# Letting the first expert's blocks start ahead of the last row's scatters, and writing later experts' pads between experts

## The chip, the cores and the metric

The kernel runs on one core of a Trainium2 chip. The metric is the device time of one execution in microseconds (us), taken as the median of several runs. Engines are named as in the profile: PE (TensorE), DVE (VectorE), ACT (ScalarE), POOL (GpSimd), SP (SyncE); a "q" behind a name (SPq, ACTq) is that engine's instruction queue, which also issues DMAs and reads registers.

## The reference

Everything is in float32, on x of 8 batch rows x 512 tokens x 128. Four parts follow one another, each of them added to x:

```python
x = x + attn_a(layernorm(x))          # 16 heads of 64, causal softmax
x = x + ffn(layernorm(x))             # mixture of experts, below
x = x + attn_b(layernorm(x))          # linear attention, 8 heads of 128, then a gated MLP
x = x + ffn(layernorm(x))             # the same mixture, the same weights

def ffn(x):                            # E = 8 experts, the best K = 2 of each token
    xn = layernorm(x) * gamma + beta
    scores, idx = top_k(softmax(xn @ Wr + br), 2)
    full = [relu(xn @ W1[e] + b1[e]) @ W2[e] + b2[e] for e in range(8)]   # 128 -> 512 -> 128
    c = relu(b1) @ W2 + b2                                              # one vector per expert
    out = sum over the 2 chosen of scores * (full[idx] - c[idx] + c.sum())
    return x + out
```

So the mixture runs twice in one execution. Each time 4096 tokens x 2 choices = 8192 token rows are spread over 8 experts, unevenly.

## The kernel before

The kernel computes only the chosen experts. Each token's row of 130 floats (128 of data, the token's number and its first expert) is **scattered** to a DRAM buffer `expert_in`, in which every expert has a region of its own (`REGION` = 4352 rows). POOL does this with indirect DMAs, 8 for each batch row (`Route.pool_scatter_one`, L674 to L677). The semaphores `scattered[u]` count what has landed; batch row b uses number b mod ring (ring 2 in the first mixture, 3 in the second), so the last row, 7, shares number 1 with other rows in both.

When the last row is routed, PE sums the counts of all experts with one matmul (`pe_count`, L914), and DVE makes the plan of them (`dve_plan`, L921): where each region ends (`fill_at`) and how many blocks of 256 rows each expert has (`blocks`). The last block of an expert is rarely full. So ACT writes 256 rows of padding behind each region's end, one DMA of 130 KB per expert (`fill`, L940), each with its own semaphore `filled[e]`; all eight are issued ahead of ACT's part of the experts.

Then every engine runs `each_block` (L896): for each expert in turn a hardware loop over its blocks. Only SP reads an expert's number of blocks as it comes to it (L900); PE, ACT, DVE and POOL read all eight numbers beforehand (`load_counts`, L889 to L894). For one block:

- SP loads it from `expert_in` to the one tile `xb` (L955), once the block before it is transposed and its token numbers are copied. SP is thus about two blocks ahead of ACT.
- PE, in this order: the matmuls to the hidden layer (L979), the transposes of the *next* block (L973), the matmuls back (L989). A wait in L973 holds up L989 of the block before it.
- ACT applies relu (L1000), DVE copies the meta columns (L1011), scales the transposed block (L1015) and adds the constant (L1035), and POOL scatters the result to `expert_out` (L1047).

SP's waits are `rows_written` (L958), all scatters of all rows, once before the first block, and `pads_written(e)` (L962), the pad of expert e, ahead of that expert's blocks.

In the first mixture DVE, PE and ACT also fold weights for the next stage between the plan and the experts (`Folding`): for DVE these are `dve_c`, `dve_const`, then `load_counts`, then `dve_last` (L831 to L846), which ends with two copies of the experts' constants (L841) and the subtraction that makes `WVO_lo` (L845). PE waits for L841's second copy before its experts. In the second mixture nothing stands between the plan and the experts but `load_counts`. POOL's `pool_work` begins with `prime` (L470), two small DMAs whose landing it waits for.

## Time and profile before

| | us |
|---|---|
| median of 3 runs (lowest, highest) | 1390.03 (1387.22, 1393.89) |
| the profiled execution, time | 1388.27 |
| its span | 1386.4 |
| PE, DVE, ACT, POOL busy in the span | 1232.6, 925.7, 822.6, 516.3 |

How to read it: the span is cut into stages by the instructions' lines. Attention a runs from 0 to about 541 us, the last row's routing and the folding to 577, the first mixture's experts to about 712, linear attention to about 1050, the MLP and the routing to 1214, the second mixture's experts to about 1359, and the last combination to the end. The shares of busy time are averages over stages with different limits. In the rows further down, a line of the timeline gives the start, the length of the piece, the engine, the line of the kernel, what is written from what, how many instructions, and in brackets how long the engine had been idle before it and what ended that. "issue" there is time in which the engine's queue itself was at work or waited for nothing that the profile shows.

### The profile page before, as it was taken

How to read it: one execution, taken by the hardware profiler on the slowest of the kernel's cores; microseconds unless marked ns; L12 is line 12 of the kernel's file. 1: busy time of each engine (PE TensorE's matmuls, PEld its weight loads, DVE VectorE, ACT ScalarE, POOL GpSimd, SP SyncE). 2: the span in 40 equal slices, each digit the busy share in tenths (PEclk: the TensorE clock that was granted, in tenths of full speed). 3: DMA queues.
4: the chain of work that ended last, by engine and by line, in shares of the span. 5: the costliest groups of instructions: out<-in, count | busy, mean ns of one | idle time of the engine just before them, and what ended most of it. 6: DMA issues, size and time to landing. Idle time of an engine off the chain costs nothing. (4 is left out here: it accounts for less than half of the span.)

```text
span 1386.4 us, 27110 instructions
## 1 busy us (share of the span) xinstructions
PE 1232.6 (89%) x7787; PEld 930.6 (67%) x7787; DVE 925.7 (67%) x3602; ACT 822.6 (59%) x2478; POOL 516.3 (37%) x683
## 2 busy tenths in 40 slices
PE   6999999999999998699958999999997988199990
PEld 5666666666666666499945777777774655189990
DVE  6778888888888776344436888888773555344445
ACT  5888888888888885244423555555654654044440
POOL 2112333342424233355532344434332455535451
PEclk9999999999999999799988999999998998589995
DMA  9100000000000000222220000000000011222225
GB/s 283 47 1 1 9 9 9 9 9 11 11 8 13 7 13 11 72 69 71 70 89 16 16 17 16 16 1 1 1 1 1 24 32 33 64 63 73 68 71 189
DMA packets 54445, 52.92 MB, mean 38 GB/s; under 512 B 7341, under 2 KB 43098, under 8 KB 54330
## 3 DMA queue, kind: packets, MB, share of 16 engines
q1 hardware_dynamic: 36320, 29.39, 7.3%
q0 software_dynamic: 8928, 17.84, 3.8%
q10 hardware_dynamic: 9082, 4.33, 1.1%
q8 instruction: 52, 0.85, 0.3%
q14 instruction: 63, 0.52, 0.1%
HBM read 29.48 MB, written 22.05 MB: 37 GB/s over the span
## 5 line engine op out<-in xcount | busy, mean ns | idle before, releaser
L1350 ACT ACTIVATE prob<-prob,negmax 128x512 f32<-128x512 f32 (+3 forms) x512 | 283.0, 556 | 78.7 <-DVE negmax L1449 76.7
L1449 DVE CUSTOM_DVE_ANT_0 prob<-bank,mask 128x512 f32<-128x512 f32 (+3 forms) x512 | 227.8, 483 | 51.0 <-PE bank L1159 50.7
L1526 POOL TENSOR_TENSOR Vs<-Vh_sb,rinv 128x256 f32<-128x256 f32 x128 | 78.2, 611 | 364.1 <-DVE rinv L1426 363.9
L1047 POOL DMA_INDIRECT expert_out<-f_x_yb,f_x_to x142 | 136.1, 958 | 155.1 <-DVE f_x_yb L1035 88.0
L1176 PE MATMUL bank<-prob,Vs 128*64 128x512 f32 (+3 forms) x1024 | 151.9, 439 | 0.9 <-DVE zT_lo L1421 0.9
L675 POOL DMA_INDIRECT expert_in<-f_xn,f_slot x128 | 127.0, 993 | 47.7 <-issue 29.3
L979 PE MATMUL bank<-f_x_xbT,W_sb 128*128 128x256 f32 x568 | 138.5, 388 | 1.6 <-DVE f_x_xbT L1015 1.5
L1000 ACT ACTIVATE f_x_hid<-bank,cols 128x256 f32<-128x256 f32 x144 | 63.4, 473 | 93.0 <-PE bank L979 93.0
L979 PEld LDWEIGHTS bank<-f_x_xbT,W_sb 128*128 128x128 f32 x568 | 104.6, 194 | 14.8 <-DVE f_x_xbT L1015 3.0
L1176 PEld LDWEIGHTS bank<-prob,Vs 128*64 128x64 f32 x1024 | 63.4, 136 | 69.4 <-issue 59.5
L1000 ACT ACTIVATE prob<-bank,cols 128x256 f32<-128x256 f32 x140 | 61.0, 473 | 81.7 <-PE bank L979 79.5
L1032 DVE CAST f_x_to<-f_x_this_to 128x1 int32<-128x1 f32 x142 | 21.4, 150 | 116.2 <-DMA expert_out<-f_x_yb,f_x_to 115.8
L1350 ACT ACTIVATION_READ_ACCUMULATOR prob<-prob,negmax 128x1 f32 x512 | 97.1, 190 | 0.0
L1159 PE MATMUL bank<-Q_hi,K_hi 64*128 64x512 f32 (+3 forms) x512 | 93.1, 357 | 2.8 <-DVE K_lo L1416 2.1
L1943 DVE SCALAR_TENSOR_TENSOR z_sb<-bank,ro,z_sb 128x128 f32<-128x128 f32 x256 | 88.4, 345 | 6.4 <-POOL ro L1877 2.9
L1809 ACT ACTIVATE yT_hi<-bank 128x512 fp32r<-128x512 f32 x64 | 38.2, 598 | 91.5 <-PE bank L1736 91.5
L451 PE MATMUL bank<-WVO_hi,yT_hi 128*128 128x256 f32 x256 | 74.8, 292 | 10.9 <-DVE z_sb L1943 10.9
L1816 ACT ACTIVATE junk<-bank 128x128 f32<-128x128 f32 x256 | 68.4, 273 | 26.8 <-PE bank L453 15.4
L1159 PE MATMUL bank<-Q_hi,K_lo 64*128 64x512 f32 (+3 forms) x512 | 83.4, 319 | 0.0
L1159 PE MATMUL bank<-Q_lo,K_hi 64*128 64x512 f32 (+3 forms) x512 | 83.2, 318 | 0.0
L1159 PEld LDWEIGHTS bank<-Q_hi,K_hi 64*128 64x128 f32 x512 | 48.4, 183 | 44.3 <-issue 34.2
L452 PE MATMUL bank<-WVO_lo,yT_hi 128*128 128x256 f32 x256 | 72.2, 282 | 0.0
(263 smaller groups left out, 3204.5 us busy)
## 6 DMA issues: line engine op xcount, KB each, us to landing
f_x_xb<-expert_in SPq DMA_DIRECT2D x73, 130.0 KB
b_crows<-expert_out SPq DMA_DIRECT2D x16, 256.0 KB, 2.8
c_crows<-expert_out SPq DMA_DIRECT2D x16, 256.0 KB, 3.9
expert_out<-f_x_yb,f_x_to POOLq DMA_INDIRECT x142
expert_in<-fill ACTq DMA_DIRECT2D x16, 130.0 KB, 2.4
x_sb<-in_L_attn_a_x_dram SPq DMA_DIRECT2D x8, 256.0 KB, 6.7
W_sb<-in_L_ffn_W_dram SPq DMA_DIRECT2D x1, 2048.0 KB, 10.8
expert_in<-f_xn,f_slot POOLq DMA_INDIRECT x128
```

Source lines behind the costliest of these rows:

```text
L451: nc.tensor.matmul(ps, lhsT_hi, rhs_hi, start=True, stop=False)
L452: nc.tensor.matmul(ps, lhsT_hi, rhs_lo, start=False, stop=False)
L675: pool.indirect_dma_start(xg, bass.IndirectOffsetOnAxis(ap=self.slot[:, u, t, k:k + 1], axis=0), self.norm.xn_sb[:, u, t, :], None).then_i ...
L979: nc.tensor.matmul(self.bankH[c][:, 0:BLK], W1_sb[:, e, c * P:(c + 1) * P], self.xbT[:, :], start=True, stop=True).then_inc(self.up_done[c ...
L1000: nc.scalar.activation(self.hid[:, c, :], self.bankH[c][:, 0:BLK], ACT.Relu, bias=b1_col[:, e * FC + c:e * FC + c + 1]).then_inc(self.hid_ ...
L1047: pool.indirect_dma_start(yg, bass.IndirectOffsetOnAxis(ap=self.to[:, t:t + 1], axis=0), self.yb[:, t, :], None).then_inc(self.stored[t], 16)
L1159: mm = nc.tensor.matmul(bankS[which][a][:, 0:width[i]], left[r, g % 2, tile], right[r, g % 2, 0:width[i]], start=(right is Q_hi and left i ...
L1176: mm = nc.tensor.matmul(bankZ[heads, 0:width[tiles_of(m)[which]]], Vs[:, m % 4, AT[which], heads], prob[:, m % 4, a, columns_of(m, which)] ...
L1350: nc.scalar.activation(mine, mine, ACT.Exp, scale=-1.0, bias=negmax[:, n % 4, t, a:a + 1], accum_out=rowsum[:, n % 4, t, a:a + 1]).then_in ...
L1449: nc.vector.tensor_tensor_reduce(out=prob[:, n % 4, a, columns_of(n, which)], in0=bankS[which][a][:, 0:width[i]], in1=mask[:, T - width[i] ...
L1526: nc.gpsimd.tensor_tensor(Vs[:, m % 4, :, :].rearrange("p t (a d) -> p t a d", a=2), V_sb[:, quarter % 2, small:big + 1:big - small, pair] ...
L1943: nc.vector.scalar_tensor_tensor(out=tile, in0=bankO[s % 2 * 2 + m // 2][:, o:o + D], scalar=ro[:, s % 2, m:m + 1], in1=tile, op0=ALU.mult ...
```

## The change

- **Early loads of expert 0.** PE also sums the last row's own counts (four more matmuls in `pe_count`). DVE works out from them how many of expert 0's blocks are full without that row (`dve_early`, five small instructions behind `dve_plan`). SP reads this number. It waits for all scatters but the last row's before the first block; blocks from that number on wait for the last row and for expert 0's pad, by a wait on a computed value, and expert 1 waits for the last row in any case.
- **Pads between experts.** Ahead of the experts ACT writes only the pads of experts 0 and 1. The pad of expert e+1 is issued when ACT begins expert e, for e from 1 to 6. Two semaphores (even and odd experts) take the place of eight.
- **Moves.** The subtraction for `WVO_lo` goes from the end of `dve_last` to just behind the last row's normalisation on DVE, and PE's last wait counts one more. The two primes of `pool_work` go to the primes at the beginning of each stage.

```diff
             def pe_count(self, pe, route):
                 pe.wait_ge(route.run_ready, START + 2 * B + 2)
                 pe.wait_ge(route.slot_ready, START + B)
+                for t in range(NT):
+                    nc.tensor.matmul(route.bankR[:, E:2 * E], ones_bf[:, :], route.sel[:, t, :],
+                                          start=(t == 0), stop=(t == NT - 1))
                 nc.tensor.matmul(route.bankR[:, 0:E], ones_bf[:, :], run_bf[:, :], start=True,
                                  stop=True).then_inc(self.counted, 1)
...
+            def dve_early(self, dve, route):
+                dve.wait_ge(self.plan_step, 1)
+                nc.vector.tensor_tensor(self.limit[:, 0:1], self.counts[:, 0:1], route.bankR[:, E:E + 1],
+                                        ALU.subtract).then_inc(self.plan_step, 1)
+                dve.wait_ge(self.plan_step, 5)
+                nc.vector.tensor_scalar(self.limit[:, 1:2], self.limit[:, 0:1], 1.0 - BLK, None,
+                                        ALU.add).then_inc(self.plan_step, 1)
+                dve.wait_ge(self.plan_step, 6)
+                nc.vector.tensor_tensor(self.whole[:, :], self.limit[:, 1:2].to_broadcast([P, MAX_BLOCKS]),
+                                        full_blocks[:, :], ALU.is_gt).then_inc(self.plan_step, 1)
+                dve.wait_ge(self.plan_step, 7)
+                nc.vector.tensor_reduce(self.limit[:, 0:1], self.whole[:, :], AX.X, ALU.add).then_inc(self.plan_step, 1)
+                dve.wait_ge(self.plan_step, 8)
+                nc.vector.tensor_copy(self.early[:, :], self.limit[:, 0:1]).then_inc(self.early_ready, 1)
...
             def sp_work(self, sp, route):
-                begin(sp, self.loaded)
+                begin(sp, self.loaded, *self.filled)
                 sp.wait_ge(self.plan_ready, 2)
+                sp.wait_ge(self.early_ready, 1)
+                early = sp.value_load(self.early[0:1, 0:1], min_val=0, max_val=MAX_BLOCKS)
...
-                def rows_written():
+                def first_rows_written():
                     for u in range(route.ring):
-                        sp.wait_ge(route.scattered[u], PRIMED + len(range(u, B, route.ring)) * 16 * TOP * NT)
-
-                def pads_written(e):
-                    sp.wait_ge(self.filled[e], 16)
+                        sp.wait_ge(route.scattered[u], PRIMED + (rows_of[u] - (u == of_last)) * one_row)
+
+                def all_rows_written(e):
+                    if e == 1:
+                        sp.wait_ge(route.scattered[of_last], PRIMED + rows_of[of_last] * one_row)
+                    if e >= 1:
+                        sp.wait_ge(self.filled[e % 2], START + 16 * (e // 2 + 1))
+
+                def block_load(e, i, row, k):
+                    if e == 0:
+                        late = i >= early
+                        sp.wait_ge(route.scattered[of_last], late * one_row + (PRIMED + (rows_of[of_last] - 1) * one_row))
+                        sp.wait_ge(self.filled[0], late * 16 + START)
+                    load(row, k)
...
             def act_work(self, act, n):
...
+                def fill_next(e):
+                    if 1 <= e < E - 1:
+                        self.fill(act, range(e + 1, e + 2))
 
-                self.each_block(act, n, relu)
+                self.each_block(act, n, relu, None, fill_next)
...
             def pool_work(self, pool, n):
-                prime(pool, *self.stored)
...
-                    experts.fill(act, range(0, 3))
+                    experts.fill(act, range(0, 2))
                     folding.act_third(act)
-                    experts.fill(act, range(3, E))
...
                     route.dve_normalise(dve, B - 1, 1)
+                    folding.dve_Wv(dve)
...
                     experts.dve_plan(dve, route)
+                    experts.dve_early(dve, route)
...
-                        experts.fill(act, range(E))
+                        experts.fill(act, range(0, 2))
```

## Rows read from the trace of the kernel before

**Rows 1.** Windows view, the first mixture's experts: stretch, length, busy times, clock, DMA share, GB/s

```profile
core 0: us, PE busy (x) PEld busy (x) DVE busy (x) ACT busy (x) POOL busy (x), PEclk, DMA share, GB/s
576.80:712.00 135.20, 134.18 (x909) 122.84 (x910) 60.36 (x280) 61.00 (x140) 64.91 (x68) 0.98 0.24 67
```

**Rows 2.** Waits of SP's queue from 1196 to 1216: total us, times, longest

```profile
SPq L963 <- DMA expert_in<-f_xn,f_slot: 10.7, 1, 10.7
```

**Rows 3.** Timeline of the second mixture's start

```profile
1199.91 0.17 DVE L937 TENSOR_SCALAR blocks<-f_x_nblocks 128x8 int32<-128x8 f32 x1
...
1200.82 11.60 ACTq L945 DMA_DIRECT2D expert_in<-fill  x8
...
1211.88 20.46 SPq L955 DMA_DIRECT2D f_x_xb<-expert_in  x6
1214.47 0.17 DVE L1011 COPY f_x_meta<-f_x_xb 128x4 f32<-128x4 f32 x1 [14.38 <-DMA f_x_xb<-expert_in]
...
1215.93 3.78 PE L979 MATMUL bank<-f_x_xbT,W_sb 128*128 128x256 f32 x8 [0.75 <-DVE f_x_xbT L1015]
```

**Rows 4.** Line L894, 1199 to 1218: min/median/max ns, first and last start

```profile
L894 DVEq SEQ_ASSERT  x8: 23/23/33, 1200.7 to 1205.4; - x8
L894 PEldq SEQ_ASSERT  x8: 18/18/18, 1200.8 to 1205.8; - x8
```

**Rows 5.** Timeline of the first mixture's start, 545 to 577

```profile
551.43 0.19 DVE L557 TENSOR_TENSOR f_logit<-bank,br_sb 128x32 f32<-128x32 f32 x1 [3.01 <-PE bank L547]
551.65 0.19 DVE L563 TENSOR_REDUCE f_rmax<-f_logit 128x4 f32<-128x32 f32 x1
...
555.76 0.22 PE L626 MATMUL bank<-f_sel,ones_bf 128*128 128x24 bf16 x3
...
569.02 1.29 DVE L835 SCALAR_TENSOR_TENSOR WVO_lo<-bank,WVO_hi 128x512 fp32r<-128x512 f32 x2 [4.15 <-issue]
...
572.15 0.69 DVE L841 COPY moe_const<-bank 128x512 f32<-128x512 f32 x1 [0.81 <-PE bank L762]
572.76 1.22 DVE L845 TENSOR_TENSOR WVO_lo<-z_sb,WVO_hi 128x1024 fp32r<-128x1024 f32 x1
...
576.80 0.29 PEld L973 LDWEIGHTS bank<-ident,f_x_xb 128*128 128x128 f32 x2 [6.31 <-DMA f_x_xb<-expert_in]
```

**Rows 6.** SP's count reads and block loads, 682 to 690, then 1331 to 1339

```profile
L894 SPq TENSOR_LOAD <-blocks x3: 5/15/367, 682.2 to 689.6; - x3
...
L955 SPq DMA_DIRECT2D f_x_xb<-expert_in x2: 18/148/278, 684.9 to 688.1; - x2
...
L894 SPq TENSOR_LOAD <-blocks x2: 264/418/573, 1331.3 to 1335.0; - x2
...
L955 SPq DMA_DIRECT2D f_x_xb<-expert_in x3: 373/373/377, 1330.6 to 1338.0; - x3
```

**Rows 7.** Line L907 on ACT: where it enters an expert's loop, in each mixture

```profile
L907 ACTq MOVE  x1: 35/35/35, 687.4 to 687.4; - x1
...
L907 ACTq MOVE  x1: 35/35/35, 1337.3 to 1337.3; - x1
```

**Rows 8.** Line L945, the pads' DMAs, 560 to 578, then 1199 to 1216

```profile
DMA to landing us min/median/max: 2.1/2.2/2.4
...
DMA to landing us min/median/max: 3.3/3.3/3.3
```

**Rows 9.** Timeline of the first mixture's experts 5 and 6

```profile
689.02 1.89 PE L979 MATMUL bank<-f_x_xbT,W_sb 128*128 128x256 f32 x8
...
690.75 0.38 PE L973 MATMUL bank<-ident,f_x_xb 128*128 128x128 f32 x2
...
692.75 1.89 PE L979 MATMUL bank<-f_x_xbT,W_sb 128*128 128x256 f32 x8
693.39 1.77 ACT L1000 ACTIVATE prob<-bank,cols 128x256 f32<-128x256 f32 x4 [1.97 <-PE bank L979]
```

**Rows 10.** Windows view in linear attention: the clock behind a short stop of PE

```profile
1037.00:1039.80 2.80, 0.65 (x4) 0.46 (x4) 1.81 (x5) 0.60 (x1) 0.69 (x1) 1.00 0.00 0
1039.80:1043.20 3.40, 3.40 (x19) 3.40 (x18) 1.60 (x5) 1.25 (x8) 0.49 (x2) 0.50 0.01 2
```

More of the change, by code:

```diff
@@ L763, in pe_last @@
                                      start=True, stop=True).then_inc(self.moe_done, 1)
-                pe.wait_ge(self.low, 4)
+                pe.wait_ge(self.low, 5)
                 pe.wait_ge(self.moe_copied, 2)
@@ L805, in dve_scale, with dve_Wv @@
                                         ALU.mult).then_inc(self.scaled, 1)
+            def dve_Wv(self, dve):
+                dve.wait_ge(self.Wv_hi_ready, 1)
+                nc.vector.tensor_tensor(WVO_lo[:, :, 0:DB], Wv_sb.rearrange("p (h v) -> p h v", v=DB),
+                                        WVO_hi[:, :, 0:DB], ALU.subtract).then_inc(self.low, 1)
             def dve_c(self, dve):
@@ L853, in __init__ @@
                 self.over = sb(name + "_x_over", [P, E, MAX_BLOCKS], at=at)
+                self.limit, self.early = sb(name + "_x_limit", [P, 2], at=at), sb(name + "_x_early", [P, 1], i32, at=at)
+                self.whole = sb(name + "_x_whole", [P, MAX_BLOCKS], at=at)
+                self.early_ready = sem(name + "_x_early_ready", at)
                 self.nblocks = sb(name + "_x_nblocks", [P, E], at=at)
@@ L857, in __init__ @@
                 self.plan_ready = sem(name + "_x_plan_ready", at)
-                self.filled = [sem(f"{name}_x_filled{e}", at) for e in range(E)]
+                self.filled = [sem(f"{name}_x_filled_{of}", at) for of in ("even", "odd")]
                 self.xb = sb(name + "_x_xb", [P, BT, W], at=at)
@@ L974, in transpose, with expert @@
                     mm.then_inc(self.transposed, 1)
-                def expert(e, row, k, k16):
+                def expert(e, k, k16):
                     pe.wait_ge(self.xbT_ready, k + 1)
@@ L995, in act_work, with relu @@
             def act_work(self, act, n):
-                def relu(e, row, k, k16):
+                def relu(e, k, k16):
                     act.wait_ge(self.down_done[BT - 1], k)
@@ L1040, in pool_work, with store @@
             def pool_work(self, pool, n):
-                prime(pool, *self.stored)
-                def store(e, row, k, k16):
+                def store(e, k, k16):
                     for t in range(BT):
@@ L1518, in _ @@
                     ahead.pool_rstd(pool, 0, 0)
-                    prime(pool, *route.scattered)
+                    prime(pool, *route.scattered, *experts.stored)
                     def scale_V(b, m):
@@ L2191, in _ @@
                         experts.dve_plan(dve, route)
+                        experts.dve_early(dve, route)
                         experts.dve_work(dve, experts.load_counts(dve))
```

19 lines of the change are left out of this document (11 added, 8 removed).

## The prediction

> **What bounds the kernel now.** I read the table of stages first. The change touches only the two mixtures, and within them two kinds of place: the start, and the borders between experts. The windows view shows the experts themselves bound by PE, busy 134.18 of 135.20 us in the first mixture [rows 1]. A gain can only come from starting that PE stream earlier, and anything that holds the stream up later costs its full length.
>
> I then read the start of the second mixture, the cleaner one. The plan is ready at 1200.08 (L937, 1199.91 + 0.17), but the first block's load is issued at 1211.88 and its meta columns are copied at 1214.47 [rows 3]. In between SP waits 10.7 us for the last row's scatters [rows 2]. This is the wait that the change removes. The first mixture shows the same: PE's transposes start at 576.80 after 6.31 us idle, ended by the load's DMA [rows 5]. There DVE folds weights until 572.84 (L841, 572.15 + 0.69), so only about 4 us can be won at all.
>
> Last I read how far apart ACT and SP are at the borders of experts, because a pad is now issued by ACT at one border and awaited by SP at the next.
>
> **Part 1, what is added behind the plan.** Four matmuls of 8 columns: three of at most 24 columns took 0.22 us [rows 5], so 0.3 us before the plan. Five dependent DVE instructions at the pitch of the small ones, 551.43 to 551.65, 0.22 us each [rows 5]: 1.1 us. Together early_ready comes 1.4 us after the old plan. The least it can be is 1.0, as the first of the five need not wait for the plan's last.
>
> **Part 2, the second mixture's start.** SP: early_ready at 1200.08 + 1.4 = 1201.5. Before, the end of SP's wait (about 1210.9; the load's issue lies 1.0 behind it, since the count is read in between) led to the issue at 1211.88 [rows 3]. A second value read costs what one of L894's costs: on PE and DVE the last of eight starts its end marker 5.0 and 4.7 us after the first one's [rows 4], seven reads, so 0.7 each. The compare and the computed waits are not in the trace; between 0.2 and 0.8 us, I take 0.4. Issue at 1201.5 + 1.0 + 0.7 + 0.4 = 1203.6, landing 1214.47 - 1211.88 = 2.6 later [rows 3]: 1206.2.
>
> What is late next are the count reads themselves. PE ends its eight at 1205.8 and DVE at 1205.4 [rows 4], until now hidden under SP's wait. PE's move by 0.3 to 1206.1, DVE's stand behind dve_early and move by 1.4 to 1206.8. PE's first matmul of the block came 1.46 after the meta copy (1215.93 against 1214.47 [rows 3]); its own part of that is transposes that PE can start at 1206.3 while DVE still reads. I take 1207.8 for the first L979, against 1215.93: **8.1 us gained**. If PE waited for DVE's last read too it would be 7.6; with landing at 1207 it is still 7.6. ACT is free in time: two pads, then eight reads of 0.6 to 0.7, from 1200.4, end near 1207.5, and relu is due near 1208.6. In the early blocks nothing waits again: the scatters land near 1210.9 as before, and with a first block starting at 1207.8 the third load is not due before about 1211.
>
> **Part 3, the first mixture's start.** The folding sets it. DVE's dve_early (1.1) and PE's matmuls (0.3) stand before dve_c, so L841's last copy ends at up to 572.84 + 1.3 = 574.1, because the eight reads ahead of L835, which show as 4.15 us of "issue" [rows 5], move with it. PE's transposes start 0.2 behind, at 574.4 against 576.80: **2.4 us gained**. The subtraction L845, 1.22 us, no longer stands behind L841; in its new place it falls into the 3.01 us for which DVE waits for the logits before L557 [rows 5], which hides it. If that gap were not there it would cost 1.22 us on the routing's chain, and the gain here would halve. The load lands around 567, well before. The primes leave a place between POOL's last scatter and its first store, which waits for a whole block's work, and go to the stages' beginnings, where POOL feeds nothing that is due soon: nothing either way.
>
> **Part 4, the pads between experts.** Six times in each mixture ACT reads a value and issues a DMA at a border. From the plan to the first pad's issue it is 1200.82 - 1200.08 = 0.74 us, and eight took 11.60, up to 1.45 each [rows 3]. ACT is idle 1.97 us before each block's relu [rows 9], which hides it. Without that cover it would cost up to 12 x 1.45 = 17 us.
>
> Where SP stands matters more. SP loads about two blocks ahead of ACT, and expert e+1's pad is issued only when ACT begins expert e. With three blocks in e or more, the pad has landed in time. Experts with one block don't give it that time. SP's count reads and loads show which these are: from 682.2 to 689.6 SP reads the counts of experts 5, 6 and 7, and issues only two loads, 684.9 and 688.1, so experts 5 and 6 have one block each; in the second mixture expert 6 has one (reads at 1331.3 and 1335.0, one load between, and expert 7's first at 1338.0) [rows 6].
>
> First mixture: ACT enters expert 5's loop at 687.4 [rows 7], issues pad 6 at 687.4 + 0.7 = 688.1, it lands 2.2 later [rows 8], 690.3, and SP issues the load 1.0 after that, at 691.3, against 688.1 before [rows 6]: 3.2 late. The load before had landed just in time for the transposes (L973's matmuls at 690.75, its weights 0.2 earlier [rows 9]), so PE stops for about 3.2 us, and L989 of expert 5, queued behind L973, stops too. Pad 7 is issued at ACT's next border, 687.4 + 3.7 + 0.7, lands at 694.0, its load is issued at 695.0, landed 697.4: by then PE is itself 3.2 late, at 694.5 + 3.2 = 697.7, so it costs nothing more. Second mixture: ACT at 1337.3 [rows 7], pad 7 at 1338.0, landed 1340.2, load 1341.2 to 1341.3 against 1338.0 [rows 6]: 3.3 late. **Cost 6.5 us** for both. An expert of two blocks (expert 5 there) has one block pitch more, 692.75 - 689.02 = 3.73 [rows 9], and just escapes; between 0 and 0.5 us, I take 0.
>
> The stop also reaches the clock. In linear attention PE, at full speed, was busy only 0.65 of 2.80 us; in the next 3.40 us the granted clock was 0.50, the 1.2 GHz level [rows 10]. A stop of 3.2 us should do the same, and 3.4 us at half speed lose up to 1.7. Part of it need not fall under PE work: 1.5 each, bounds 0 and 3.4. **Cost 3.0 us.** The Trainium skill ("TensorE: Matmul & The Clock Gate", section "HAM oscillation — how this bites in real kernels") likewise says that a wait for data between bursts of matmuls sends TensorE back to half rate; the trace agrees, and by it alone the change could lose more than it wins (second rival).
>
> Another page speaks against Part 2. The one pad timed while the last row's scatters ran took 3.3 us to land, those of the first mixture 2.2 [rows 8]. An early load now runs among the scatters; at 3.3 it lands at 1206.9 and costs some 0.5 us. The Trainium skill ("DMA: Bandwidth & Descriptors", section "Issuing engines are not separate DMA queues") says that DMAs of all issuing engines interleave on the same 16 DMA engines. By it the gain is 7.6, by the undisturbed 2.6 us 8.1.
>
> **Sum**: -8.1 - 2.4 + 6.5 + 3.0 = -1.0 us on the profiled execution's 1388.27 (span 1386.4 and 1.9 around it): 1387.3. The median of the runs lies 1.8 above that execution, so I predict 1390.0 - 1.0 = 1389.0 us.
>
> **The rivals.**
> - **No stops.** Pads land before SP needs them, if ACT runs further ahead of the relus than I read. For it: ACT is idle half of each block. Against it: ACT's queue enters a loop only after the last relu's issue, and rows 7 give those times. Only the starts would remain: -10.5, 1379.5 us. 12%.
> - **The clock turns it.** The starts win 10.5, the stops themselves cost 6.5, so the change becomes slower once each stop loses more than 2.0 us by the clock. It does if PE stays at the 1.2 GHz level for more than 4 us of work. For it: at the start of the experts the first eight L979 took 3.78 us against 1.89 later [rows 3, 9], so low stretches longer than one block exist. Against it: in rows 10 it ended after 3.4 us. With 6.8 us low at each, -10.5 + 6.5 + 6.8 = +2.8: 1393 us, slower than before. 15%.
> - **ACT's cover fails.** Eight pads took 11.60 where 1.1 each would be 8.8: ACT's queue also stalls. A pad that takes over 2 us at a border delays its relus and with them PE. With 0.5 us at each of 12 borders: +5, 1395 us. 6%.
> - **It doesn't do what it says.** If SP still waits for the last row (no block is early, or the computed wait is taken wrongly), the starts win nothing but the stops stay: +9.5 + 1, about 1400. 5%.
>
> **How the numbers follow.** My forecast has 62%; its own range is 1384 to 1392: the clock's bounds (-3.0 to +1.5 or so), 1 us for Parts 2 and 3, and the spread of the runs of before. The range reaches towards both sides, 1381 to 1395. A measurement of this kernel can tell about 0.5%, 7 us, from no change. Faster than 1383.1: the first rival, 12%, and 1% of the forecast. Slower than 1397: the last rival, 5%, and 1% of the third. Else the same: 81%.
>
> **What the profile would show.** Right: SP's first load near 1203.6 - and the first L979 near 1207.8 - on before's scale; the eight reads as the last thing before it; in the first mixture the first transposes at 574.4 behind L841; L973 with a wait of about 3 us on the load's DMA once in each mixture, where a single-block expert is followed by another; the granted clock at 0.50 shortly behind. Wrong: no such wait, or one at every short expert; a relu of ACT that starts later than 0.7 us behind L979 at borders; a first load that still follows the last scatter.

## The result, and the profile after

The changed kernel takes **1399.35 us** (median of 6 runs, 1396.23 to 1400.98), the kernel before 1390.06 beside it (1387.22 to 1393.89): a ratio of 1.0065, 95% interval 1.0044 to 1.0085. The forecast was 1389.0 with a range up to 1395. So it was wrong, and wrong in the sign.

The profiled execution took 1400.98 us with a span of 1399.1, against 1388.27 and 1386.4. PE is busy for 1230.6 us of it, before 1232.6, so the 12.7 us more are not added work but waiting. One of the twelve runs of wv_primes_back below took 2461.59 us; its ratio leaves that run out. To see where they come from, I measured both traces from the same marks: the last row's exp (L574 on ACT), the instant DVE copies the counts out of PSUM, the first up-matmul (weights of L979 before, L1021 after), and the last block's first up-matmul.

| us | before | after | difference |
|---|---|---|---|
| last row's exp to first up-matmul, first mixture | 26.14 | 34.28 | +8.1 |
| first to last block, first mixture | 130.28 | 136.41 | +6.1 |
| last row's exp to first up-matmul, second mixture | 21.21 | 14.83 | -6.4 |
| first to last block, second mixture | 134.49 | 142.05 | +7.6 |
| all the rest | | | -2.7 |

**First mixture's start.** The timeline of after, DVE (start, length, engine, line, output<-input, idle before and its releaser):

```profile
548.99 1.21 DVE L809 TENSOR_TENSOR WVO_lo<-z_sb,WVO_hi 128x1024 fp32r<-128x1024 f32 x1
556.49 0.17 DVE L661 CAST f_slot<-f_slotf 128x8 int32<-128x8 f32 x1
571.48 0.17 DVE L935 COPY f_x_counts<-bank 128x8 f32<-128x8 f32 x1 [14.82 <-remote]
573.34 0.15 DVE L965 CAST f_x_early<-f_x_limit 128x1 int32<-128x1 f32 x1
582.38 1.50 DVE L846 COPY moe_const<-bank 128x512 f32<-128x512 f32 x2
```

and PE there:

```profile
559.98 0.18 PE L929 MATMUL bank<-run_bf,ones_bf 128*128 128x8 bf16 x1 [0.54 <-issue]
574.14 0.58 PE L748 MATMUL bank<-c_sb,ones 8*8 8x128 f32 x2 [13.98 <-DVE b_c L817]
584.21 0.66 PE L1015 MATMUL bank<-ident,f_x_xb 128*128 128x128 f32 x2 [1.05 <-DVE moe_const L846]
585.60 0.80 PE L1021 MATMUL bank<-f_x_xbT,W_sb 128*128 128x256 f32 x1 [0.74 <-DVE f_x_xbT L1062]
```

The counts' matmul is recorded at 559.98, and DVE sees its result only at 571.48, 11.5 us later. The releaser reads "remote": the trace names nothing that ended the wait. Everything behind it moves, the plan, the folding, L846 and the transposes. What was running in these 11.5 us stands on POOL, the scatters of the last two rows (after):

```profile
547.66 1.07 POOL L675 DMA_INDIRECT expert_in<-f_xn,f_slot  x1 [0.40 <-issue]
549.03 2.01 POOL L675 DMA_INDIRECT expert_in<-f_xn,f_slot  x1 [0.30 <-issue]
...
557.67 0.96 POOL L675 DMA_INDIRECT expert_in<-f_xn,f_slot  x1 [0.31 <-issue]
558.94 0.96 POOL L675 DMA_INDIRECT expert_in<-f_xn,f_slot  x1 [0.30 <-issue]
...
567.80 0.96 POOL L675 DMA_INDIRECT expert_in<-f_xn,f_slot  x1 [0.30 <-issue]
```

Sixteen of them follow one another without a gap and end at 568.76. Before, there was a gap between the eight of row 6 and the eight of row 7 (POOL, before):

```profile
548.38 0.96 POOL L675 DMA_INDIRECT expert_in<-f_xn,f_slot  x1 [0.30 <-issue]
...
555.96 0.96 POOL L675 DMA_INDIRECT expert_in<-f_xn,f_slot  x1 [0.31 <-issue]
560.57 0.96 POOL L675 DMA_INDIRECT expert_in<-f_xn,f_slot  x1 [3.65 <-DVE f_slot L661]
```

**Second mixture's start**, the part that went roughly as forecast (DVE, SP's queue and PE, after; the rows of before are [rows 3]):

```profile
1213.12 0.15 DVE L965 CAST f_x_early<-f_x_limit 128x1 int32<-128x1 f32 x1
1219.28 0.70 SPq L987 DMA_DIRECT2D f_x_xb<-expert_in  x1
1220.15 0.17 DVE L1058 COPY f_x_meta<-f_x_xb 128x4 f32<-128x4 f32 x1 [6.88 <-DMA f_x_xb<-expert_in]
1221.60 2.93 PE L1021 MATMUL bank<-f_x_xbT,W_sb 128*128 128x256 f32 x6 [0.74 <-DVE f_x_xbT L1062]
```

**The stops** at the single-block experts are there, one in each mixture (PE, after):

```profile
703.48 0.44 PE L1015 MATMUL bank<-ident,f_x_xb 128*128 128x128 f32 x2 [2.54 <-DMA f_x_xb<-expert_in]
703.76 3.23 PE L1031 MATMUL bank<-W_sb,prob 128*128 128x128 f32 x16
...
1352.60 0.63 PE L1015 MATMUL bank<-ident,f_x_xb 128*128 128x128 f32 x2 [3.02 <-DMA f_x_xb<-expert_in]
1353.03 3.43 PE L1031 MATMUL bank<-W_sb,f_x_hid 128*128 128x128 f32 x16
```

SP's waits (source line, what was waited for, total us, times, longest), from 690 to 706 and from 1340 to 1356, show that each load came late because of its pad:

```profile
SPq L899 <- DMA expert_in<-fill: 2.4, 1, 2.4
...
SPq L899 <- DMA expert_in<-fill: 2.8, 1, 2.8
```

PE waits 2.5 and 3.0 us, and the sixteen matmuls behind each wait take 3.23 and 3.43 us instead of the 1.95 they take elsewhere: the clock. The windows view (busy time and count for each engine, then the granted clock, the DMA share and GB/s) has it at 0.67 and 0.54 of full speed over 3.4 us, a mix of the 1.2 GHz and the 2.4 GHz level:

```profile
703.00:706.40 3.40, 2.92 (x17) 2.92 (x18) 1.12 (x5) 0.00 (x0) 0.16 (x1) 0.67 0.24 68
1353.00:1356.40 3.40, 3.40 (x19) 3.40 (x18) 0.95 (x4) 0.00 (x0) 0.29 (x1) 0.54 0.21 44
```

The longest pitches (from one block's first up-matmul to the next one's) are 7.63 and 8.60 us, where 3.73 is the rule [rows 9].

**The blocks behind the other pads** take 3.73 to 4.69 us. At the longest of them, ACT is not late: its relu starts 0.74 us behind the up-matmul, as in any block. What comes late is the landing of the previous block's result scatter, for which DVE waits before it copies the next addresses (POOL, ACT's queue with the pad, ACT and DVE, after):

```profile
614.28 0.96 POOL L1093 DMA_INDIRECT expert_out<-f_x_yb,f_x_to  x1 [1.06 <-issue]
616.80 0.15 DVE L1079 CAST f_x_to<-f_x_this_to 128x1 int32<-128x1 f32 x1 [1.73 <-DMA expert_out<-f_x_yb,f_x_to]
617.99 0.96 POOL L1093 DMA_INDIRECT expert_out<-f_x_yb,f_x_to  x1 [1.12 <-DVE f_x_yb L1082]
618.02 0.45 ACTq L972 DMA_DIRECT2D expert_in<-fill  x1
619.46 1.77 ACT L1042 ACTIVATE prob<-bank,cols 128x256 f32<-128x256 f32 x4 [1.97 <-PE bank L1021]
621.67 0.15 DVE L1079 CAST f_x_to<-f_x_this_to 128x1 int32<-128x1 f32 x1 [2.89 <-DMA expert_out<-f_x_yb,f_x_to]
```

One block earlier it is 2.52 us from the scatter's issue to DVE's copy; with a pad issued beside the scatter it is 3.68. Away from the stops four blocks behind a pad take over 4.1 us, and all four have 3.4 to 3.7 us there.

### The profile page after: what moved, and what is told of

Read it like the earlier page. It is cut to its first block and busy times, and to the rows that moved or that the text cites. A ratio compares the mean times of both kernels' runs of the same rounds, so it can differ in the third digit from the quotient of the medians.

```text
span 1399.1 us, 27171 instructions
## 1 busy us (share of the span) xinstructions
PE 1230.6 (88%) x7795; PEld 928.6 (66%) x7795; DVE 928.2 (66%) x3612; ACT 823.8 (59%) x2478; POOL 517.9 (37%) x683
## 5 line engine op out<-in xcount | busy, mean ns | idle before, releaser
L1021 PE MATMUL bank<-f_x_xbT,W_sb 128*128 128x256 f32 x568 | 139.5, 390 | 2.1 <-DVE f_x_xbT L1062 2.0
L1021 PEld LDWEIGHTS bank<-f_x_xbT,W_sb 128*128 128x128 f32 x568 | 105.0, 195 | 15.8 <-DVE f_x_xbT L1062 3.5
L1205 PEld LDWEIGHTS bank<-Q_hi,K_hi 64*128 64x128 f32 x512 | 48.4, 183 | 44.3 <-issue 34.3
L1031 PE MATMUL bank<-W_sb,f_x_hid 128*128 128x128 f32 x576 | 72.2, 280 | 0.2 <-ACT f_x_hid L1042 0.2
```

What stands on the lines that cost most here:

```text
L1021: nc.tensor.matmul(self.bankH[c][:, 0:BLK], W1_sb[:, e, c * P:(c + 1) * P], self.xbT[:, :], start=True, stop=True).then_inc(self.up_done[c ...
L1031: mm = nc.tensor.matmul(self.bankY[t][:, 0:D], self.hid[:, c, t * P:(t + 1) * P], W2_sb[:, e, c, :], start=(c == 0), stop=(c == FC - 1))
L1205: mm = nc.tensor.matmul(bankS[which][a][:, 0:width[i]], left[r, g % 2, tile], right[r, g % 2, 0:width[i]], start=(right is Q_hi and left i ...
```

## The experiments

Marks as in the table above, in us, from each kernel's one profiled execution, which can lie some us off the median (scatter_waits 1395.32, pause_mid 1398.43, wv_only 1391.06); "counts" is the time from the last row's exp to DVE's copy of the counts. The ratio is to the kernel before, run beside it. Beside the experiments that kernel took 1387.37 to 1388.59 us in the median, so the rows are compared by their ratios. The edits below show the lines that count.

| kernel | counts, 1st | start, 1st | experts, 1st | start, 2nd | experts, 2nd | median us | ratio (95%) |
|---|---|---|---|---|---|---|---|
| before | 8.4 | 26.1 | 130.3 | 21.2 | 134.5 | 1390.06 | |
| after | 20.2 | 34.3 | 136.4 | 14.8 | 142.1 | 1399.35 | 1.0065 (1.0044-1.0085) |
| wv_only | 19.8 | 32.6 | 130.5 | 21.1 | 134.3 | 1393.63 | 1.0042 (1.0028-1.0057) |
| wv_back | 8.3 | 24.1 | 134.6 | 15.4 | 142.1 | 1390.43 | 1.0012 (1.0000-1.0025) |
| first_late | 20.1 | 32.9 | 136.8 | 14.9 | 140.7 | 1396.62 | 1.0048 (1.0031-1.0066) |
| scatter_waits | 8.9 | 24.3 | 138.5 | 14.9 | 141.9 | 1389.90 | 1.0016 (1.0005-1.0026) |
| pause_mid | 14.5 | 29.7 | 137.6 | 14.8 | 142.4 | 1393.39 | 1.0044 (1.0028-1.0060) |
| only_pads_between | 9.2 | 25.7 | 134.5 | 20.6 | 138.9 | 1395.07 | 1.0056 (1.0040-1.0071) |
| pads_front | 20.1 | 34.0 | 130.7 | 15.4 | 142.3 | 1397.00 | 1.0049 (1.0027-1.0071) |
| two_ahead | 19.9 | 34.3 | 133.1 | 14.4 | 141.2 | 1395.47 | 1.0043 (1.0030-1.0056) |
| prime_only | 9.1 | 26.9 | 129.2 | 21.5 | 137.0 | 1387.72 | 0.9997 (0.9987-1.0008) |
| wv_primes_back | 9.2 | 24.1 | 135.6 | 14.7 | 141.7 | 1388.01 | 1.0008 (0.9995-1.0021) |
| two_ahead_wait | 8.8 | 24.0 | 134.3 | 14.4 | 138.8 | 1385.60 | 0.9982 (0.9973-0.9991) |
| best_primes_back | 8.8 | 24.1 | 132.4 | 14.7 | 138.8 | 1383.53 | 0.9974 (0.9964-0.9984) |
| pads_first1 | 8.9 | 24.4 | 135.8 | 14.8 | 138.4 | 1389.35 | 1.0006 (0.9991-1.0021) |
| scatters_behind_load | 8.4 | 23.9 | 132.4 | 13.0 | 146.0 | 1390.06 | 1.0013 (1.0003-1.0023) |

They are told in the order of the argument.

### What holds the counts' signal: scatter_waits, first_late, pause_mid

Scatter_waits is the changed kernel with one more wait on POOL:

```diff
                     route.pool_scatter(pool, B - 2, 0)
+                    pool.wait_ge(experts.counted, 1)
                     route.pool_scatter(pool, B - 1, 1)
```

> The changed kernel; in the first mixture GpSimd does not start the last row's scatters before the counts' matmul has been signalled, one wait on GpSimd. In the changed kernel that matmul is recorded at 559.98 us and VectorE sees it at 571.45, 2.7 us after the last of GpSimd's scatters. Theory 1 (TensorE's signals are held while GpSimd issues indirect DMAs in a row): with the wait the counts are seen by about 561 to 562 us, the plan is ready by 563, the scatters run until 572 or so but the first blocks do not need them, and the first up-matmul comes 6 to 10 us earlier than 585.6; the time is 1389 to 1393. Theory 2 (the hold is TensorE's own, its instructions come late there whatever GpSimd does): the counts are seen at 571 or so all the same, then the scatters start only there and the first mixture's last row lands 11 us later, while early blocks hide it; the time stays 1399 to 1403.

DVE, scatter_waits:

```profile
561.06 0.17 DVE L935 COPY f_x_counts<-bank 128x8 f32<-128x8 f32 x1 [3.59 <-PE bank L929]
```

The counts come at 561.06, the start falls by 10 us to 24.3 us behind the exp, the time to 1389.90. Theory 1 holds, theory 2 falls.

First_late leaves the four added matmuls, DVE's five steps and the early loads out of the first mixture:

```diff
-                for t in range(NT):
+                for t in range(NT if self.by_early else 0):
```

> The changed kernel without the early loads in the first mixture: there all loads wait for the last row's scatters as in the kernel before, and the four matmuls that count the last row and the five VectorE steps behind them are left out; the second mixture and the pads stay as changed. Theory 1 (the hold of the counts' signal meets any kernel whose counts' matmul falls inside GpSimd's last-row scatters): VectorE still sees the counts at about 571 us, and the first up-matmul stays at 584 to 586; the time is 1398 to 1401. Theory 2 (the four added matmuls bring the hold about): the counts are seen at 560 to 561 and the first up-matmul comes at 577 to 579 as before; the time is 1391 to 1393.

The counts are late by the same amount (20.1). The added work of the early loads does not cause it; theory 2 falls. The time, 1396.62 us, lies 1.4 below what theory 1 gave.

Pause_mid puts the same wait in the middle of the last row's scatters:

```diff
-                    route.pool_scatter(pool, B - 1, 1)
+                    route.pool_scatter(pool, B - 1, 1, 0, 4)
+                    pool.wait_ge(experts.counted, 1)
+                    route.pool_scatter(pool, B - 1, 1, 4)
```

> The changed kernel; in the first mixture GpSimd issues four of the last row's eight scatters, waits for the counts' signal, and issues the other four. Theory 1 (TensorE's signals are held until the run of indirect DMAs pauses, whatever is left to scatter): the run pauses after 12 scatters, near 563.7 us, and the counts are seen 1.6 to 2.7 us behind the end of the twelfth, at 565.3 to 566.5 us, 14 to 15 us after the exp; the time is 1393 to 1396. Theory 2 (the signal needs the end of all scatters, or a fixed time): it would be seen at 560 to 562 or hang behind it past 568; a fixed hold of 11 us gives 571.

The matmul is recorded at 559.80, the last scatter ahead of the pause begins at 562.62 (POOL, then DVE, pause_mid):

```profile
562.62 0.96 POOL L675 DMA_INDIRECT expert_in<-f_xn,f_slot  x1 [0.30 <-issue]
565.94 0.96 POOL L675 DMA_INDIRECT expert_in<-f_xn,f_slot  x1 [2.36 <-remote]
```

```profile
565.70 0.17 DVE L935 COPY f_x_counts<-bank 128x8 f32<-128x8 f32 x1 [8.46 <-remote]
```

565.70 is 2.1 us behind the twelfth scatter's end. It lies inside what theory 1 gave, and neither a fixed hold nor a wait for all scatters fits. Across the kernels the counts are seen 2.7 us (after), 2.1 (pause_mid), 2.4 (wv_only, below) and 1.6 (scatter_waits) behind the end of the run of scatters in which the matmul fell.

### What made the scatters one run: wv_only, wv_back

Wv_only is the kernel before with the shift of WVO_lo's first half alone, wv_back the changed kernel without that shift:

```diff
                     route.dve_normalise(dve, B - 1, 1)
+                    folding.dve_Wv(dve)
                     for n in ROUTE_DVE:
```

> The kernel before with one piece of the change: WVO_lo's first half is computed by VectorE before the last row's routing steps and no longer behind the constants (the wait for low parts counts 5). Theory 1 (this shift of VectorE's work brings the last row's slots early enough that GpSimd scatters the last two rows without a gap, and so brings about the held signal): the counts are seen 19 to 20 us after the last row's exp, the first load stays near because it waits for the scatters anyway, the plan is late by 11 us, and the first up-matmul comes 31 to 34 us after the exp: 1393 to 1397 us. Theory 2 (it is harmless): counts 8 to 9 us after the exp, 1387 to 1390 us.

> The changed kernel with WVO_lo's first half computed at its old place, behind the constants; all else as changed. If this one shift brought about the held counts' signal, VectorE sees the counts 8 to 9 us after the last row's exp instead of 20, the first up-matmul comes 24 to 26 us after it instead of 34.3, and the time is 1390 to 1392 (stops and borders still cost 10 to 12 us, the starts win 6.4 and up to 2). If it is not this shift alone, the counts come at 20 us again and the time is 1396 to 1400.

Wv_only, POOL and DVE:

```profile
548.06 2.01 POOL L675 DMA_INDIRECT expert_in<-f_xn,f_slot  x1 [0.30 <-issue]
```

```profile
570.17 0.17 DVE L926 COPY f_x_counts<-bank 128x8 f32<-128x8 f32 x1 [14.55 <-remote]
```

Wv_back, POOL and DVE:

```profile
548.21 0.96 POOL L675 DMA_INDIRECT expert_in<-f_xn,f_slot  x1 [0.30 <-issue]
...
560.39 0.96 POOL L675 DMA_INDIRECT expert_in<-f_xn,f_slot  x1 [3.64 <-DVE f_slot L661]
```

```profile
560.40 0.17 DVE L933 COPY f_x_counts<-bank 128x8 f32<-128x8 f32 x1 [0.85 <-PE bank L927]
```

The shift alone brings the late counts and costs 5.8 us (1.0042); taking it alone out of the change takes them away and brings the ratio from 1.0065 to 1.0012, some 7 us. Theory 1 of wv_only and the first of wv_back's two expectations hold. How it does this can be followed in the rows. The subtraction runs on DVE from 548.99 to 550.20 (after), and the scatter that begins beside it takes 2.01 us instead of 0.96; so it is in all eleven kernels with the shift, and in none of the five without. Row 6's scatters thus take 1 us longer. And the last row's slots are ready at 556.7 instead of 559.7, because in the kernel before that chain was itself caught. There PE's L628 is recorded at 555.83, row 6's scatters end at 556.92, and DVE goes on only at 558.75 (DVE, before):

```profile
558.75 0.19 DVE L636 TENSOR_TENSOR f_place<-bank,region_at 128x32 f32<-128x32 f32 x1 [2.85 <-remote]
```

That hold of 2.9 us made the gap in POOL's scatters, and the gap let the counts through. With the shift the chain escapes (L636 at 555.68), the gap closes, and the next signal of PE is held until the end. In all five kernels without the shift L636 is held like this, after 2.85 to 5.13 us of idle DVE; with it in only one of eleven, scatters_behind_load (4.12). That one shows that the shift does not always free the chain. How one longer scatter lets it through is not shown by any run.

The Trainium skill ("SBUF — State Buffer", section "Who interferes with whom") says that a VectorE instruction with both inputs in SBUF contends with a GpSimd instruction that reads SBUF. The stretched scatter agrees with it: L809 has two such inputs, and the scatter became 1.05 us longer. The same section also tells of a test in which an instruction of this kind (`tensor_tensor`) did not stall a DMA; here the DMA's instruction on POOL was stretched, and the measurement decides.

### The pads: only_pads_between, pads_front, two_ahead

Only_pads_between is the kernel before with the pads between experts and two semaphores; pads_front is the changed kernel with all pads up front:

```diff
-                self.each_block(act, n, relu, None, fill_next)
+                self.each_block(act, n, relu)
```

> The kernel before with one part of the change alone: pads of experts 2 to 7 are issued between experts and two semaphores count the pads. Theory 1 (pads between experts cost the stops, the long wait of VectorE for the counts in the first mixture has nothing to do with them): the two mixtures last 3.5 and 4.4 us longer at the single-block experts and the first mixture starts as before, 1396 to 1400 us. Theory 2 (pads up front were themselves in the way of the first loads): the starts of both mixtures win 1 us or more and the time is 1393 to 1396. Theory 3 (stops are not the pads'): 1390.

> The changed kernel with all pads of later experts issued ahead of the expert loops again, as in the kernel before (the pads of the last two experts share one semaphore); everything else as changed. Theory 1 (stops of 3.5 us in the first mixture and 4.4 us in the second, at the block after the last single-block border, come from the pads made between experts): first up-matmul to last up-matmul falls from 136.4 us to about 131 to 133 in the first mixture and from 142.1 to 135 to 138 in the second, and the time falls from 1399.4 to about 1391. If the small losses at the other borders go with the pads too, the stretches are the 130.3 and 134.5 of the kernel before and the time is about 1386. Theory 2 (the stops are not the pads' but those of the loads' new wait on the loop counter or of the clock): the stretches stay within 2 us of the changed kernel's and the time within 2 us of 1399.

The pads alone cost 7.8 us (1.0056). The time, 1395.07 us, is 0.9 below theory 1's and inside theory 2's range, but the starts win only 0.4 and 0.6 us, not the 1 of theory 2. The stops appear in both mixtures without any early load, pitches of 8.16 and 6.66 us, and three borders of longer experts take 4.4 to 4.8. Theory 1's mechanism holds there. In pads_front the stops go (behind the first block no pitch of the first mixture is over 4.20 us, and its experts last 130.7), but the second mixture does not win. ACT and PE, pads_front:

```profile
1223.39 1.57 ACT L1042 ACTIVATE f_x_hid<-bank,cols 128x256 f32<-128x256 f32 x4 [21.59 <-issue]
```

```profile
1215.42 3.78 PE L1021 MATMUL bank<-f_x_xbT,W_sb 128*128 128x256 f32 x8 [0.74 <-issue]
1219.22 0.61 PE L1015 MATMUL bank<-ident,f_x_xb 128*128 128x128 f32 x2
1224.38 3.76 PE L1031 MATMUL bank<-W_sb,f_x_hid 128*128 128x128 f32 x16 [4.55 <-ACT f_x_hid L1042]
```

ACT issues eight pads and then reads eight counts, and its first relu comes 8 us behind the first up-matmul; the second block follows 12.3 us behind the first instead of 6. Neither theory had this. With an early start, pads up front and early loads are in each other's way. Of this kernel's twelve runs nine took 1395.4 to 1399.7 us and three 1385.9 to 1390.4, more spread than any other; the profiled one has the late counts.

Two_ahead issues each pad two experts ahead, on four semaphores:

```diff
-                    if 1 <= e < E - 1:
-                        self.fill(act, range(e + 1, e + 2))
+                    if 1 <= e < E - 2:
+                        self.fill(act, range(2 if e == 1 else e + 2, e + 3))
```

> The changed kernel with the pads still made between experts but two experts ahead (pads of experts 2 and 3 at the second expert's start, then that of expert e+2 at the start of expert e), on four semaphores. Theory 1 (the stops are SyncE waiting for a pad that was asked for one single-block expert before): the pitches of 7.63 and 8.60 us fall to 4.2 or less in both mixtures, first to last up-matmul falls to 131 to 134 and 135 to 138 us, the late counts of the first mixture stay; the time is 1390 to 1393. Theory 2 (the stops come from ScalarE's own time for the pad, which delays its relus): the stops move to the border where two pads are issued and the time stays 1397 to 1400.

The longest pitches fall from 7.63 and 8.60 to 4.80 and 5.21. The ratio falls from 1.0065 to 1.0043, 3 us of the 6 to 9 expected, and the two intervals overlap. In the traces the two stops lose 7.7 us less and the other blocks 3.3 more: those behind a pad take 3.9 to 5.2 us. Theory 2, ACT's own time, does not explain this. At the two longest, 4.80 and 5.21 us, the relus start 0.74 and 0.88 us behind the up-matmul, and from the last result scatter's issue to DVE's copy it is 4.1 and 4.4 us, as behind the pads of the changed kernel. Where two pads are issued at one border, the relus do start 0.2 to 0.5 us later.

### The primes: prime_only, wv_primes_back

Prime_only primes the stores' semaphores early in the kernel before; wv_primes_back undoes both side moves in the changed kernel.

```diff
-                    prime(pool, *route.scattered)
+                    prime(pool, *route.scattered, *experts.stored)
```

> The kernel before with another piece of the change: the semaphores of the stores are primed by GpSimd at the start of each stage, with those of the scatters, and not ahead of the stores. Theory 1 (this is only a shift of two small DMAs and does not touch the last row): counts 8 to 9 us after the exp, the start of both mixtures as before or up to 1 us earlier, 1387 to 1389 us. Theory 2 (GpSimd's start is shifted, its second scatter takes 2.0 us as in the changed kernel, and the counts' signal is held): counts 19 to 20 us after the exp, 1393 to 1397 us.

> The changed kernel with both side moves undone: WVO_lo's first half behind the constants again, the primes ahead of the stores again. What is left is what the change is named for, early loads and pads between experts. Against the kernel with only the first half moved back (1390.4 us): Theory 1 (the early primes slow the middle of the second mixture): 2 us less there, 1388 to 1389. Theory 2 (they do nothing): 1390 to 1391, and the second mixture's slow blocks stay.

The primes do not touch the counts (9.1) and cost nothing (0.9997). The time of wv_primes_back is what theory 1 gave, but the rows that it rested on are against it. Blocks of 3.82 to 4.35 us in the second mixture number eleven in wv_primes_back and ten in wv_back, so the early primes are not needed for them. But there are ten in prime_only too, against four before, and its second mixture's experts last 2.5 us longer in the profiled execution. There are eight in after and three in wv_only. One trace for each kernel does not settle what part the primes have. In after, DVE's copies come 2.7 to 3.3 us behind the result scatters' issue in the five slow blocks from 1277 to 1298 us, where 2.3 to 2.6 is usual: what comes late there is again the landing. Why it does stays open.

### A better version: two_ahead_wait, best_primes_back, pads_first1, scatters_behind_load

Two_ahead_wait joins two_ahead and the wait of scatter_waits; best_primes_back puts the primes back besides.

> The kernel of pads two ahead, and GpSimd's last-row scatters of the first mixture wait for the counts' signal as well. If the costs found so far (late counts 9 to 10 us, stops 3.5 and 4.4 us or more) are separate and all of the loss, both starts win what was forecast (about 1.8 and 6.4 us against before) and the experts last 131 to 134 and 135 to 138 us: 1380 to 1384 us, against 1388.6 before. If something else takes their place (ScalarE's relus late by the pads, borders of all experts slower by 0.5 us each), 1385 to 1389.

> The kernel of pads two ahead with the wait of the last-row scatters (1385.6 us), with the stores' semaphores primed ahead of the stores again, as in the kernel before. In all kernels with the early primes, that with the primes alone too, five to eight blocks in the middle of the second mixture came at 3.9 to 4.3 us instead of 3.73, without them two or three did. Theory 1 (the early primes bring this about): the second mixture's experts lose 2 us less, 136.5 instead of 138.8, and the primes cost at most 0.5 at the start, which lies under other waits: 1383 to 1384.5 us. Theory 2 (the slow blocks have another cause): 1385 to 1388.

1385.60 us (0.9982) and **1383.53 us** (0.9974, 0.9964 to 0.9984). The second is 0.26% faster than the kernel before, some 3.6 us, and the best of all. Two_ahead_wait missed its 1380 to 1384: the starts win what was expected, but the second mixture's experts last 138.8 us. Best_primes_back has the time of theory 1, but not by its mechanism: the second mixture's experts last 138.8 us as well, with seven slow blocks. The two intervals overlap, so the primes' part in the gain is not shown. In best_primes_back the early load still sets the second mixture's start (PE):

```profile
1206.51 0.69 PE L1015 MATMUL bank<-ident,f_x_xb 128*128 128x128 f32 x2 [9.05 <-DMA f_x_xb<-expert_in]
```

Pads_first1 is two_ahead_wait with the first mixture's pads up front:

> The kernel of pads two ahead with the wait of the last-row scatters (1385.6 us), but in the first mixture all pads are issued up front as before (those of the last two experts share a semaphore). The first mixture's experts lasted 134.3 us with pads two ahead and 130.7 with pads up front. Theory 1 (up front nothing is paid, ScalarE is idle there): 1381 to 1383 us. Theory 2 (eight pads and the count reads make ScalarE's first relu late, as in the second mixture of the kernel with all pads up front, where the second block came 12.3 us behind the first): the first pitch grows by 2 us or more and the time is 1384 to 1388.

Theory 2, and somewhat more than it gave (1389.35): the second block follows 8.8 us behind the first (ACT and PE, pads_first1).

```profile
581.63 1.57 ACT L1047 ACTIVATE prob<-bank,cols 128x256 f32<-128x256 f32 x4 [9.80 <-issue]
```

```profile
582.61 3.15 PE L1036 MATMUL bank<-W_sb,prob 128*128 128x128 f32 x16 [2.25 <-ACT prob L1047]
```

Scatters_behind_load lets the second mixture's last-row scatters wait for the first load:

```diff
+                        pool.wait_ge(experts.loaded, START + 16)
                         route.pool_scatter(pool, LAST, slot_of(LAST))
```

> The kernel of pads two ahead with the wait of the first mixture's last-row scatters (1385.6 us); in the second mixture GpSimd's last-row scatters wait too, until the first block's load has landed. In the kernels so far SyncE's and ScalarE's instructions come at 0.7 us each from 4 us after those scatters have begun, and the first load is recorded 11.7 to 12.5 us after the exp although the plan is ready at 6.5. Theory 1 (the scatters slow the other queues): the load is issued by 9.5 and the first up-matmul comes 12 to 13 us after the exp instead of 14.4, 1 to 2 us gained: 1383.5 to 1385; the last row's scatters end 5 us later and may hold a later block of expert 0 back, which would show as a long pitch among the first six. Theory 2 (the 0.7 us are the queues' own): the load stays at 11.7 and the time grows by what the late scatters cost, 1386 to 1390. The form works only where expert 0 has a block without the last row.

Theory 1 holds for the load: issued 8.8 us behind the exp instead of 11.7, first up-matmul at 13.0 instead of 14.4. Its time, 1383.5 to 1385 us, does not come. The scatters then run from 1206.99 to 1216.79 beside the first blocks, and the third block comes 9.7 us behind the second (PE and ACT, scatters_behind_load):

```profile
1218.60 1.57 ACT L1042 ACTIVATE f_x_hid<-bank,cols 128x256 f32<-128x256 f32 x4 [6.58 <-remote]
1219.58 3.75 PE L1031 MATMUL bank<-W_sb,f_x_hid 128*128 128x128 f32 x16 [4.12 <-ACT f_x_hid L1042]
```

ACT's relu, which needs signals of matmuls recorded between 1213.35 and 1215.24, starts 1.8 us behind the last scatter's end, and PE goes on behind it. The hold moved from the start into the experts; 1390.06 us.

## Why the prediction was wrong, point by point

- **Part 3, the step that failed.** "in its new place it falls into the 3.01 us for which DVE waits for the logits before L557 [rows 5], which hides it." On DVE it does: the logits' addition L557 follows it by 0.44 us. But I costed only the engine that it runs on. It stretched a scatter of POOL's and moved the last row's slots ahead of the end of row 6's scatters, and what followed cost 5.8 us alone and some 7 in the whole change. The forecast had 0, and 1.22 as its worst. The hold was in the rows of before, DVE's "2.85 <-remote" at 558.75, and I had not asked what ended it.
- **Part 3, the rest.** Without the held signal the first mixture starts 1.7 to 2.3 us earlier (23.9 to 24.4 behind the exp against 26.1, in the kernels with early loads), forecast 2.4, and by the forecast's path: PE's transposes behind the last copy of `moe_const`.
- **Part 1.** early_ready is set 0.8 us behind the plan (1212.47 and 1213.27), forecast 1.4, least 1.0: the chain overlaps the plan's last steps further than I counted.
- **Part 2.** 6.4 us gained, forecast 8.1. From early_ready to the meta copy it takes 6.9 us, forecast 4.7. The view of SP's load by source line (count; shortest, median, longest in ns) shows a step ahead of the issue at 700 ns in after and at 56 in scatters_behind_load, where the scatters come later; there DVE's wait is 5.3 us:

```profile
L987 SPq FUSED_REGOPS  x2: 46/373/700, 1217.9 to 1223.1; - x2
```

```profile
L987 SPq FUSED_REGOPS  x1: 56/56/56, 1203.7 to 1203.7; - x1
```

  So the scatters beside the load cost most of the difference. They do it by slowing the queue that issues it, not by the landing that I had priced at 0.5. The record of the issue, at 1219.28, is itself late: the windows view (clock, DMA share, GB/s at the end of the row) has data moving before it, after a stretch with none:

```profile
1218.50:1218.90 0.40, 0.00 (x0) 0.00 (x0) 0.00 (x0) 0.00 (x0) 0.32 (x1) 0.50 0.00 0
1218.90:1219.20 0.30, 0.00 (x0) 0.00 (x0) 0.00 (x0) 0.00 (x0) 0.08 (x1) 0.50 0.60 47
```

  From early_ready to the load's first data it is 5.6 us here and 3.2 in scatters_behind_load. Start times of queue instructions in such stretches are thus to be read with care.
- **Part 4, the stops.** Forecast 6.5 + 3.0 us for waits and clock. In after, the two pitches are 8.8 us over their values before (3.73 each); the waits are 2.5 and 3.0 us, forecast 3.2 and 3.3, and the sixteen matmuls behind them 1.3 and 1.5 us longer, forecast 1.5. The experts with one block are those read from SP's count reads. This step was right.
- **Part 4, the other borders.** Forecast 0 to 0.5 us, hidden by ACT's idle 1.97 us. Measured: 3.9 us more than before for all blocks but the first and the stops, over both mixtures, 1.4 us with the pads alone. Blocks behind a pad take up to 4.7 us where 3.73 is due, and the slow blocks of the second mixture are in this number. ACT's cover held, the relus come on time, so the third rival is not what cost this. The step that was missing is the landing of the result scatters, 3.4 to 3.7 us beside a pad instead of 2.5; that the pad's transfer delays it is read from the coincidence, no run separates it.
- **The sum.** What the change is named for, early loads and pads between experts, gives 1388.01 us, ratio 1.0008 (wv_primes_back), +1.1 us where -1.0 was forecast. Of that the pads cost 7.8 (forecast 9.5), so the early loads win some 7 (forecast 10.5), 8.5 at the starts less what the blocks behind them lose. The whole change cost 9.0 us by its ratio, 10 more than forecast. Some 7 of these came from the one shifted subtraction, the rest from the smaller gain at the second start and the slower blocks.
- **The rivals.** None had this mechanism. The last, "about 1400", gives the right number for a wrong reason: the early loads work. The second, the clock, is refuted by the 3.23 and 3.43 us.

A caution on all of this: the times of waits and borders come from one trace per kernel. Several kernels with the shift and without a wait also had faster runs (first_late one at 1389.23, two_ahead three near 1391), so the late counts need not come in every execution.

Open: why the signals are held and the queues' instructions come 0.7 us apart while POOL scatters; whether the recording of the trace takes part in it, which no run can tell; and the slow blocks in the middle of the second mixture.

## What to carry to other kernels

A piece of work moved into an idle slot of its own engine still has to be checked against what runs beside it and against the order that it changes on the others: here a 1.2 us subtraction in a real gap cost 6 to 7 us. An idle time whose releaser the profile can't name is worth explaining before anything is moved near it. A transfer asked for at one border and awaited by another engine at the next needs as much lead as that engine is ahead, and here two borders' lead did better than one (1.0043 against 1.0065) and than all pads in front (0.9982 against 1.0006, two_ahead_wait and pads_first1), though in both pairs the intervals touch or overlap.

## What the runs showed of the hardware

- While GpSimd issues indirect DMAs one after the other, signals of TensorE can be held: a matmul recorded at 559.98 was seen at 571.48. The counts were seen 2.1 to 2.7 us behind the end of the run in the six kernels with late counts, and the row places (DVE's L636) 1.3 to 1.8 us behind it in the six in which they were held. A wait that paused the run freed the counts earlier (565.70).
- In the same stretches other queues slow down: a step of SyncE's ahead of a load took 0.70 us instead of 0.06, and the load's data moved from 1218.90 on, before its issue's record at 1219.28.
- A VectorE subtraction of two SBUF tensors, 128 x 1024, 1.21 us long, stretched the indirect DMA that began beside it from 0.96 to 2.01 us.
- With a 130 KB DMA issued within 0.1 us of a block's result scatter, it took 3.68 us instead of 2.52 from the scatter's issue until DVE, which waits for its landing, went on.
- Behind stops of 2.5 and 3.0 us TensorE's granted clock was 0.67 and 0.54 over 3.4 us, and sixteen matmuls took 3.23 and 3.43 us instead of 1.95.
